# A ring of channel pairs for the mixing stages, the mask made during their first loads, and one sum moved to GpSimd

## The reference

```
h    = normalise(x)
a, b = gated projections of h                 # layer 0: sigmoid of a product of two projections
z[i, j, c] = sum over k of a[., ., c] * b[., ., c]   # one 256x256x256 product for each channel c
x    = x + gate(x) * (normalise(z over c) @ W)
```

## Time and profile before

| | us |
|---|---|
| three runs | 1714.95 median (1713.91 to 1717.31) |
| the profiled execution | 1716.62, span 1714.7 |
| busy: PE, DVE, ACT, POOL | 1435.4 (84%), 1172.3, 1050.5, 429.0 |
| stage 0 (137.3 to 194.8) | 57.5 |
| stage 1 with its mask (452.5 to 561.3) | 108.8 |
| stage 2 (885.8 to 1064.2) | 178.4 |
| stage 3 with its mask (1389.0 to 1565.5) | 176.5 |
| median landing: loads of 1 MB (stages 2 and 3; 0 and 1) | 7.8; 8.2 |
| median landing: stores of products, 512 KB | 4.9 |

### The profile page before, as it was taken

The page is one execution under the profiler, slowest core; times in us unless marked ns, Lnnn a source line. Parts: engine busy times, 40 slices in busy tenths (PEclk is TensorE's granted clock), DMA queues, the critical chain, the costliest instruction groups (busy, mean ns, idle before and its releaser), DMA issues. The chain is left out here.

```text
span 1714.7 us, 26817 instructions
## 1 busy us (share of the span) xinstructions
PE 1435.4 (84%) x9119; PEld 750.9 (44%) x9119; DVE 1172.3 (68%) x2060; ACT 1050.5 (61%) x1845; POOL 429.0 (25%) x382
## 2 busy tenths in 40 slices
PE   5796697968587697899979997998899967785987
PEld 5535432212376242133338996222233336663443
DVE  5643587179688884289957777893499956677664
ACT  4674686844234786688856666556688834444555
POOL 5400197130000594310000000792500000000665
PEclk9898899989898898999989998998899989997999
DMA  8336310026657230079987886891088878785998
GB/s 341 105 153 225 143 54 9 1 87 194 213 205 278 99 99 13 1 270 345 344 315 298 302 302 235 303 378 51 26 343 341 345 272 319 305 305 198 375 393 314
DMA packets 140872, 381.51 MB, mean 222 GB/s; under 512 B 13505, under 2 KB 13634, under 8 KB 130626
## 3 DMA queue, kind: packets, MB, share of 16 engines
q1 hardware_dynamic: 118418, 314.95, 50.4%
q10 hardware_dynamic: 22320, 64.86, 10.1%
HBM read 191.01 MB, written 188.74 MB: 221 GB/s over the span
## 5 line engine op out<-in xcount | busy, mean ns | idle before, releaser
L1350 POOL TENSOR_TENSOR xT<-xT,work 128x512 f32<-128x512 f32 x192 | 241.7, 1277 | 700.6 <-DVE work L1395 698.2
L1046 PE MATMUL bank<-work 128*128 128x256 f32 x1408 | 349.3, 401 | 59.4 <-DVE work L1112 23.9
L746 ACT ACTIVATE work<-bank,bias 128x512 f32<-128x512 f32 x448 | 286.1, 686 | 96.3 <-PE bank L645 42.0
L1046 PEld LDWEIGHTS bank<-work 128*128 128x128 f32 x1408 | 277.7, 205 | 104.5 <-DMA work<-hidden_rows 31.9
L645 PE MATMUL bank<-work,w 64*64 64x512 f32 x2048 | 257.2, 605 | 6.0 <-ACT work L742 6.0
L818 DVE SCALAR_TENSOR_TENSOR work<-bank,bias,work 128x512 f32<-128x512 f32 x320 | 236.4, 748 | 31.8 <-PE bank L645 24.2
L1069 ACT COPY work<-bank 128x512 f32<-128x512 f32 x176 | 103.3, 587 | 235.9 <-PE bank L1046 182.7
L1534 POOL TENSOR_TENSOR xT<-xT,work 128x512 f32<-128x512 f32 x64 | 80.2, 1275 | 384.4 <-ACT work L1504 384.4
L1138 DVE TENSOR_TENSOR work<-work 128x512 f32<-128x512 f32 x176 | 121.1, 688 | 71.9 <-ACT work L1069 70.5
L1395 DVE SCALAR_TENSOR_TENSOR work<-bank,bias,work 128x512 f32<-128x512 f32 x192 | 141.9, 748 | 38.2 <-ACT work L1325 22.8
L645 PEld LDWEIGHTS bank<-work,w 64*64 64x64 f32 x2048 | 84.4, 134 | 141.5 <-DVE work L818 83.0
(11 more groups left out here) (149 smaller groups left out, 2084.2 us busy)
## 6 DMA issues: line engine op xcount, KB each, us to landing
hidden_rows<-work SPq DMA_DIRECT2D x128, 512.0 KB, 3.8
work<-hidden_rows SPq DMA_DIRECT2D x60, 1024.0 KB, 7.8
products<-work ACTq DMA_DIRECT2D x88, 512.0 KB, 4.9
work<-products SPq DMA_DIRECT2D x88, 512.0 KB, 4.6
work<-gate_rows SPq DMA_DIRECT2D x64, 512.0 KB, 5.5
work<-hidden SPq DMA_DIRECT2D x18, 1024.0 KB, 8.2
work<-in_x SPq DMA_DIRECT2D x32, 512.0 KB, 4.8
gate_rows<-work SPq DMA_DIRECT2D x32, 512.0 KB, 2.7
```

Of the source, the lines that this page charges most:

```text
L746: nc.scalar.activation(result(t, column), GB[n % len(GB)][:, :], ACT.Sigmoid, bias=bias(name)).then_inc(gate_sb, 1)
L1046: mm = pe.matmul(ZB[c % 2][:, r * N:r * N + N], a[:, kk, rows_of(r)], x[:, kk, :], start=(kk == 0), stop=(kk == 1))
L1350: pool.tensor_tensor(columns(t), columns(t), term[:, t % RING, :], ALU.add).then_inc(x_sb, 1)
```

## The change

1. `mix` loads through a ring of four pairs (eight channels): pair g+4 is issued once the products of pair g are done. The first four channels are still loaded one by one, a's by SP and b's by ACT.
2. SP issues the stores of the products too, each ahead of the next loads; `zs` has OUT pairs: 3, 2, 3 and 4 in stages 0 to 3.
3. Stage 1 is one call of 32 channels.
4. `make_mask` is gone: ACT loads the mask at the head of `mix`, PE turns it there (stage 1), and stage 3 loads the row of the mask broadcast to all partitions.
5. The waits for the projections' stores stand at the head of `mix`, on SP and ACT, behind the mask's loads.
6. In stages 1 and 3, POOL adds the copies to `s1`.
7. The last two blocks fetch their first three gates before they wait for the products.

```diff
-            for b, s in enumerate(stored):
-                sp.wait_ge(s, 16 * len(range(b, PAIRS // 2, OUT)))
+    return [(s, 16 * len(range(b, PAIRS // 2, OUT))) for b, s in enumerate(stored)]
...
+    SINGLES, RING = 4, 4
+    OUT = {0: 3, 1: 2, 2: 3, 3: 4}[layer]
+    sums_on_pool = layer % 2 == 1
+    zs, at = core.area([2 * OUT, X], (2 if mask is None else 4) * X)
+    ab, at = core.area([4 * RING, X], at)
...
-            for g in range(1, channels // LOAD):
-                if nturn == 2:
-                    at_least(sp, turn_mm, 2 * LOAD * (g - 1))
-                else:
-                    at_least(sp, z_mm, LOAD * (g - 1))
-                for o in range(2):
-                    first = offsets[o] + g * LOAD
-                    sp.dma_start(to_source(slots(o, g)), source(first, LOAD)).then_inc(landed[g % 2], 16)
+            wait_rows(sp)
+            for c in range(SINGLES):
+                load_single(sp, 0, c)
+            for g in range(SINGLES // 2, RING):
+                load(g)
+            for g in range(PAIRS):
+                store(g)
+                if g + RING < PAIRS:
+                    sp.wait_ge(z_mm, 2 * g + 2)
+                    load(g + RING)
...
-                    at_least(act, stored[c // 2 % 2], 16 * (c // 4))
-                at_least(act, s1_sb, c - 3)
+                    at_least(act, stored[c // 2 % OUT], 16 * (c // 2 // OUT))
+                at_least(act, s1_sb, c - 2 * OUT + 1)
...
+            if sums_on_pool:
+                pool.memset(s1, 0.0).then_inc(s1_begun, 1)
+                pool.wait_ge(s1_begun, 1)
+                for c in range(channels):
+                    pool.wait_ge(z_sb, c + 1)
+                    at_least(pool, s1_sb, c)
+                    pool.tensor_tensor(s1, s1, zs[:, c % (2 * OUT), :], ALU.add).then_inc(s1_sb, 1)
...
+        rows = project(core, 3, "g3", "p3", "go3", ub, gmean)
-        make_mask(core, 3, mask, mask_t)
-        out = mix(core, 3, 0, 64, (0, C), (False, False), 0, 64, mask, mask_t, sums)
+        out = mix(core, 3, C, [None, (0, C)], 0, (False, False), 64, rows, mask, None, sums)
```

More of the change, by code:

```diff
@@ L868, in _ @@
                 store(u)
[L869 to L924, removed]
@@ L927, in mix @@
-def mix(core, layer, part, channels, offsets, turns, z_row, cz, mask, mask_t, sums):
+    return [(stored[s], 16 * stores * len(range(s, PAIRS, RP))) for s in range(RP)]
+def mix(core, layer, channels, offsets, turned, turns, cz, rows_out, mask, mask_t, sums):
     nc, bank = core.nc, core.bank
@@ L935, in mix @@
     shift, msq = core.fold[:, 11:12], core.fold[:, 8:10]
-    LOAD = 4
+    SINGLES, RING = 4, 4
+    OUT = {0: 3, 1: 2, 2: 3, 3: 4}[layer]
     X = 2 * N
[L938 to L941, removed]
+    PAIRS = channels // 2
+    masked_turn = layer == 1
+    row_mask = layer == 3
+    sums_on_pool = layer % 2 == 1
+    zs, at = core.area([2 * OUT, X], (2 if mask is None else 4) * X)
@@ L953, in mix @@
     TB = [[bank[0], bank[1]], [bank[2], bank[3]]]
     ZB = [bank[4], bank[5]]
-    with ExitStack() as ctx:
[L957 to L961, removed]
+    MB = bank[6]
@@ new lines, in mix, with source @@
+    nturn = sum(turns)
+    turns_of = lambda c: turns if c < turned else (False, False)
+    masked_load = lambda c: layer == 1 and c >= turned
+    def source(o, c, n):
+        first = offsets[c >= turned][o] + (c - turned if c >= turned else c)
+        return image[:, :, :, first:first + n, :].rearrange("w v h m x -> (v h) w (m x)")
+    with ExitStack() as ctx:
+        (mask_in, mask_mm, mask_sb, masked_a, masked_b, turn_mm, ta_sb, tb_sb, z_mm, z_sb, sq_sb, s1_sb, s2_sb, begun,
+         s1_begun, shifted) = core.sems(f"mix{layer}", "mask_in mask_mm mask_sb masked_a masked_b turn_mm ta_sb tb_sb z_mm z_sb "
+                              "sq_sb s1_sb s2_sb begun s1_begun shifted")
+        single = core.sems(f"mix{layer}", " ".join(f"single{c}" for c in range(SINGLES)))
+        landed = core.sems(f"mix{layer}", " ".join(f"in{n}" for n in range(RING)))
+        stored = core.sems(f"mix{layer}", " ".join(f"st{n}" for n in range(OUT)))
@@ L1155, in _ @@
             summed(channels - 1)
-    return [(s, 16 * (channels // 4)) for s in stored]
+    return [(s, 16 * len(range(n, PAIRS, OUT))) for n, s in enumerate(stored)]
 class Roots:
```

182 lines of the change are left out of this document (108 added, 74 removed).

## The result

Over all the runs beside each other the changed kernel takes 1671.0 us (1669.7 to 1672.7) and the kernel before 1714.4 (1708.8 to 1717.3): a ratio of 0.975, 95% interval 0.9725 to 0.9778. The forecast was 1670. The total came out almost exactly; several of its parts did not, and their errors cancelled.

The account below looks back on a forecast made before the run. Stage 3 was taken as bound by a two-group load ring that can't keep the DMAs full, stage 2 by PE. Stages 0 to 3 gain 11.9 + 8.7 + 1.9 + 22.7 = 45.2 us: 1670 us, range 1637 to 1689.

Parts of the forecast that it names:

- the four starts: Starts of stages 0 to 3: earlier masks, no barrier, loads issued on two queues; 2.4, 6.3, 1.9 and 5.7 us gained.
- stage 3's copies: Stage 3, first to last copy of a product: 16.9 us gained, at a pace of 2.25 us a channel.
- a ring that waits for groups of four: Stage 0 loads: eight channels with pairs issued once a pair is used should leave no stall, 2.19 us a channel.
- the third store buffer: Stage 0 stores: three buffers for two, named beside the ring for a stage without stalls; 11.9 us gained together with the start.
- DMA floor of 2.01: Stage 3: 786 kB a channel at 391 GB/s takes 2.01 us, the pace without waiting and with DMAs full.
- serial 2.34 us: Stage 3: POOL's addition and DVE's squares and row masks one after the other, 1.22 + 0.60 + 0.52 us a channel.
- the free-running rival: DVE and POOL don't hinder each other: stage 3 at 2.01 us a channel, 76 us gained, time 1639; chance 0.27.
- a DMA share below 0.95: Stage 3: a sign that would show the forecast case, DVE and POOL mostly serial at 2.2 to 2.35 us a channel.
- The first half: Stage 1, first half: only the addition of squares waits for POOL, 0 to 0.15 us a channel; 15 channels last 41.6 us.
- The second half: Stage 1, second half: 2.90 us a channel, between 2.01 free and 3.02 serial; DVE alone would have needed 2.40.
- the slower rival: Each change of owner between DVE and POOL costs time: slower from 0.145 us on, 1741 us at 0.25; chance 0.04.
- Serial with unevenness on top: DVE and POOL fully serial plus uneven DMAs: 2.45 us in stage 3, 3.10 in stage 1's second half, 1686; chance 0.12.

Follow-up runs that it names:

- the runs on the ring: Kernel with sums on DVE, loads changed: pairs freed by four, 1668.2 us; 1 MB DMAs of four channels, 1760.8 us. Changed kernel, pairs freed by four: 1684.9 us.

## Why the prediction was right, and where its parts were not

**The total: partly luck.** Against the forecast, the four starts gained 9.0 us less in the table above, stage 3's copies 7.2 us more, and the last 2.2 us were not forecast at all. Within stage 1 two errors of some 3.5 us cancel as well. What limits each stage's pace was named rightly; that the total came within 1 us was not earned.

**Stage 0: right.** Forecast 2.19 us a channel throughout, measured 2.20. The reason given, a ring that waits for groups of four, is shown by the runs on the ring; the third store buffer, given beside it, adds nothing.

**Stage 2: the pace right.** 2.60 us a channel were PE's and stayed.

**Stage 3: mechanism right, size off.** The forecast chose between a DMA floor of 2.01 and a serial 2.34 us and took 2.25. It is 2.14, which over 63 channels is 7 us more gained. The serial end counted every microsecond of DVE as held, 1.22 + 0.60 + 0.52. One of the two masks is not held: it takes 0.34 us, and the other sits through the addition. From start to start the cycle in the timeline is 0.60 (squares), 0.26 (the free mask) and 1.28 (the held one), which is 2.14. So the serial end of 2.34 counted 0.26 us too much for the free mask and 0.06 too little for the addition, and the 2.25 taken below it is still 0.11 too much. The other end was too high as well: 2.01 came from 391 GB/s of another stage, and this one moved 419 GB/s in the run with sums on DVE, a floor of 1.88. So the time of the free-running rival was put too high: 0.13 us x 63 is 8 us too much in stage 3 alone.

One sign named in advance was badly chosen: a DMA share below 0.95. Over the whole stage it is 0.92, but in its even part 0.99, although nothing waits for a load there.

**Stage 1: the total right by two errors.** The first half was to take 41.6 us for 15 channels and took 45.1; I had halved a cost of 0 to 0.15 us a channel for the addition of squares, and it is 1170 ns instead of 0.68 in the group above, which holds every second channel up by 0.58 (distances of 2.60 and 3.18 in turn). With DVE alone the distances are 2.60 throughout, but for the edges of this part, and the half takes 42.3. The second half was to take 46.4 and took 42.7, since the first four of its 16 channels still ran at 1.73 to 1.88, presumably on operands masked ahead; from the seventh on the pace is 2.90, as forecast.

**The starts: over-estimated.** One pair of profiled executions is too little for these; over the twelve new kernels and the two old ones (the kernel before, and that with the sum on GpSimd) the gaps from a last copy to the next first are:

| gap | old, two | new, mean (least to most) | difference | forecast |
|---|---|---|---|---|
| start to stage 0 | 148.5, 147.6 | 146.8 (143.3 to 149.0) | -1.3 | -2.4 |
| to stage 1 | 276.1, 276.2 | 272.8 (269.8 to 275.2) | -3.4 | -6.3 |
| to stage 2 | 339.1, 339.5 | 339.7 (336.8 to 341.9) | +0.4 | -1.9 |
| to stage 3 | 341.6, 342.5 | 337.0 (335.6 to 338.8) | -5.1 | -5.7 |

The terms of the forecast do not quite add up by themselves: 2.0 with the barrier's 0.4 is 2.4, not the 1.9 of stage 2, and 5.0 + 1.2 + 0.4 is 6.6, not 6.3.

The block for the mask did go, which is what stages 1 and 3 show: from a last copy to the next first load are 261.3 us for 266.3 at stage 1, and 328.0 for 332.6 at stage 3. The step that failed is the one by which "the first channel's second operand leaves 0.65 us sooner and the second channel's 1.3 to 2": they leave sooner, but the product does not start sooner. I priced the issue, 0.65 us each, and not what follows it. The queues at the start of stage 1, changed kernel:

```profile
439.20 0.33 ACTq L1056 DMA_DIRECT2D work<-in_L_conv_mask  x1
...
440.38 3.26 SPq L950 DMA_DIRECT2D work<-hidden  x4
443.68 2.40 SPq L956 DMA_DIRECT2D work<-hidden  x3
```

From the first load at 440.38 to the first copy at 452.37 are 12.0 us; before they were 9.9, from 457.51 to 467.4. PE turns the second channel's tiles ahead of the first product, so it needs four single loads there. The fourth lands 7.8 us after the first is issued; before it was 5.7. These are the 2.1 us given back. Splitting the issue is not the whole of it: with all eight on SP, as before, the fourth still lands after 7.1 and 7.0 us in the two kernels that ran so, and the first copy comes after 11.3 and 11.9. Over the twelve new kernels the fourth lands after 7.0 to 8.0 us, and in the two old ones after 5.7 and 6.0. Why it lands later however it is issued stays open. In stage 3, where nothing is turned, the first product needs two loads; they are there after 4.2 us for 4.4, and the first copy comes after 8.9 for 9.1.

**The rivals.** Free running is refuted by the instruction durations, and the run with sums on DVE shows what it would have been worth in stage 3. The hand-over cost of the slower rival isn't there: a cycle of 2.14 us is shorter than its parts one after the other. Serial with unevenness on top is refuted by the regular 2.14. But the prediction had the fact that mattered: it said of the second half of stage 1 that "the move to POOL costs more than it saves". It did not draw that conclusion for stage 3, where DVE alone needed 1.73 us by its own row, less than either end of the range it used. With its sum DVE was already below the DMA floor that the forecast used, so the move had nothing to gain in stage 3 even if the two engines ran freely. Setting 1.73 beside 2.01 and 2.34 would have named the fault of the change before any run.

## What to carry to other kernels

Before an addition is moved from DVE to GpSimd, compare the pace with the move to the pace without it, not to the pace of today: here DVE needed 1.73 us a channel with the addition and 2.14 without it, since GpSimd reads SBUF and holds DVE's SBUF-to-SBUF work for 1.27 us to save 0.60. When an engine waits for loads in bursts, look at how much must land before the first piece is usable and how many places are freed at once, before adding buffers or changing queues. A transfer floor is taken from the stage in question, or given a margin of the difference between stages (391 and 419 GB/s here).

## What the hardware showed that I had not expected

- A DVE instruction that is held by GpSimd is shown as busy: in stage 3 DVE reads 135.7 us busy of 138, and 0.51 us of a row mask's mean of 0.85 is waiting. A busy share near 1 with means above those of another stretch is the sign.
- It goes both ways, but unequally: POOL's addition grew from 1273 to 1359 ns in stage 3 and to 1468 in stage 1's second half, DVE's row masks from 348 to 854.
- GpSimd that only writes SBUF (memsets of 525 ns) leaves a DVE addition of two SBUF tiles at 686 ns and still lengthens a row mask to 615.
- One core moved 419 GB/s, mostly loads of 512 KB and stores of 512 KB, for 80 us with all DMA engines full.
